# One decoder layer on one core: the first feed-forward bias added by four 32-row products, one per PSUM bank, in place of four whole ones

## The reference, cut to what matters

```
x = x + ffn(layernorm(x))
def bitlinear(x, w, b):
    xn = layer_norm(x)
    scale = 127 / clip(max|xn| over the row, 1e-5)
    xq = clip(round(xn * scale), -128, 127) / scale
    wq = clip(round(w / mean|w|), -1, 1) * mean|w|
    return xq @ wq.T + b
h = gelu(bitlinear(x, w1, b1))        # w1: 2048 x 512, b1: 2048
ffn = bitlinear(h, w2, b2)            # w2: 512 x 2048
```

## Time and profile before

| what | value |
|---|---|
| median of 3 runs | 994.33 us (993.60 to 994.83) |
| profiled execution, first to last instruction | 993.8 us |
| mean granted TensorE clock | 0.953 |
| TensorE busy | 907.3 us (91%) |
| VectorE busy | 788.4 us (79%) |
| ScalarE busy | 488.8 us (49%) |
| GpSimd busy | 148.4 us (15%) |

### The profile page before, as it was taken

How to read it: one execution, slowest core, us unless ns; L and a number is a source line. 1 busy time by engine, 2 the same in 40 slices (tenths; PEclk the granted TensorE clock), 3 DMA queues, 4 the chain that set the end, 5 groups by cost and what they waited for, 6 DMA issues and landing times.

```text
span 993.8 us, 18916 instructions
## 1 busy us (share of the span) xinstructions
PE 907.3 (91%) x7673; PEld 735.2 (74%) x7690; DVE 788.4 (79%) x1205; ACT 488.8 (49%) x687; POOL 148.4 (15%) x210
## 2 busy tenths in 40 slices
PE   3467999999989999999999989999999986989996
PEld 2357988988889888898989877788878854545552
DVE  4778978879788797888848666988889789889983
ACT  4445164361643615435152343545345346879994
POOL 3000111021110211101010200000000113324431
PEclk9589899999999999999997999999999988999999
DMA  9320102012020010200504033023320421322220
GB/s 247 105 72 32 44 12 95 13 33 65 12 92 16 33 65 11 66 21 33 172 12 159 1 128 107 23 108 127 127 93 34 160 76 34 106 85 96 96 75 32
DMA packets 36951, 72.47 MB, mean 73 GB/s; under 512 B 6466, under 2 KB 7234, under 8 KB 35850
## 3 DMA queue, kind: packets, MB, share of 16 engines
q1 hardware_dynamic: 35754, 68.29, 20.5%
q0 software_dynamic: 1120, 3.10, 1.2%
HBM read 57.76 MB, written 12.58 MB: 71 GB/s over the span
## 4 chain that ended last, share of the span: by engine, by line
PE 61%; issue 16%; DVE 15%; POOL 5%; ACT 2%; DMA 1%; SPq 0%; DVEq 0%; POOLq 0%; ACTq 0%
PE S L674 11%; PE P L62 7%; PE P L63 6%; PE P L64 6%; PE S L2153 4%; PE P L2143 4%; PE S L650 3%; POOL sm L370 3%; DVE E L1738 2%; DVE xf L919 2%; PE S L1599 2%; PE P L627 1%; PE P L751 1%; PE P L760 1%; PE S L1553 1%
## 5 line engine op out<-in xcount | busy, mean ns | idle before, releaser
L674 PE MATMUL S<-R,K 64*128 64x64 f32 x1792 | 117.7, 283 | 5.1 <-DVE K L965 2.8
L674 PEld LDWEIGHTS S<-R,K 64*128 64x128 f32 x1792 | 110.1, 196 | 16.2 <-issue 10.9
L370 POOL TENSOR_TENSOR sm<-sm,mhalf 128x16 f32<-128x16 f32 x8 | 30.6, 3827 | 280.4 <-DVE sm L1012 280.4
L2153 PE MATMUL S<-wq,hqT 128*128 128x512 bf16 x255 | 62.7, 392 | 5.0 <-ACT hqT L2086 5.0
L2143 PE MATMUL P<-wq,xqT 128*128 128x512 bf16 x240 | 64.6, 390 | 2.5 <-ACT xqT L2072 1.2
L919 DVE TENSOR_TENSOR xf<-P,xx 128x1024 f32<-128x1024 f32 x40 | 48.9, 1222 | 20.4 <-PE P L627 20.4
L1738 DVE TENSOR_SCALAR E<-S,upper 128x2048 f32<-128x2048 f32 x16 | 37.6, 2350 | 29.2 <-PE S L1586 29.0
L1744 DVE RECIPROCAL rec<-S 128x512 f32<-128x512 f32 x16 | 53.6, 3352 | 2.6 <-PE S L1601 2.5
L962 DVE TENSOR_TENSOR R<-R,D 128x256 f32<-128x256 f32 x96 | 41.1, 428 | 18.1 <-PE S L674 16.5
L1412 ACT ACTIVATE E<-E 128x2048 f32<-128x2048 f32 x16 | 30.6, 1914 | 43.8 <-DVE E L1738 43.8
L2153 PEld LDWEIGHTS S<-wq,hqT 128*128 128x128 bf16 x256 | 25.1, 101 | 34.0 <-ACT hqT L2086 5.1
(11 more groups left out here) (284 smaller groups left out, 2729.6 us busy)
## 6 DMA issues: line engine op xcount, KB each, us to landing
wch<-in_wff SPq DMA_DIRECT2D x32, 256.0 KB, 3.0
cwch<-in_wff SPq DMA_DIRECT2D x8, 1024.0 KB, 6.6
xt<-in_x SPq DMA_DIRECT2D x8, 512.0 KB, 4.5
y<-in_x SPq DMA_DIRECT2D x8, 512.0 KB, 3.9
out<-y SPq DMA_DIRECT2D x8, 512.0 KB, 3.3
cxt<-out SPq DMA_DIRECT2D x8, 512.0 KB, 4.1
ct<-in_ctx SPq DMA_DIRECT2D x8, 512.0 KB, 4.9
cxr<-out SPq DMA_DIRECT2D x8, 512.0 KB, 6.6
```

What stands on the lines that cost most here:

```text
L370: pool.tensor_tensor(sm[:, 2, :], sm[:, 1, :], mhalf[:, 0:2 * H], ALU.pow).then_inc(y_rstd, 1)
L674: mm = pe.matmul(ps[:, par, b, k, :], K[head_rows(par), r % 2, T * g:T * g + T], right_tokens(par, g, i), start=True, stop=True)
L2153: mm = pe.matmul(O[:, :], hqT[b % 2][:, k, :], w2q[:, k, :], start=k == 0, stop=k == NF - 1)
```

## The change

The bias rows are laid out four times. Row group n (partitions 32n to 32n+8) of `w1b` holds the pieces of b1 for the 512 columns of bank n, so `w1b` is 512 wide and not 2048; `pieces` has the nine pieces of the reciprocal scale at columns 32n to 32n+8 for each n. `product` first makes the 16 products with the ternary weights, and then four products of 32 rows, each for its own bank. The nine DMAs of `rows()` become 36, each with a quarter of the bytes.

```diff
-    w1b = sb("w1b", [P, FF], BF16)
+    w1b = sb("w1b", [P, C], BF16)
...
             for i in range(3):
                 for j in range(3):
-                    sp.dma_start(w1b[3 * i + j:3 * i + j + 1, :], b1p[j][:, :]).then_inc(rows_in, 16)
+                    for n in range(4):
+                        at = XD * n + 3 * i + j
+                        sp.dma_start(w1b[at:at + 1, :], b1p[j][XD * n:XD * n + XD, :]).then_inc(rows_in, 16)
...
-            pc, pr = pieces[f % 2], pres[f % 2]
+            pc, pr = pieces[f % 2][:, :], pres[f % 2]
...
-                pool.tensor_copy(pc[:, 3 * i:3 * i + 3], wide(pr[:, i:i + 1], [P, 3])).then_inc(s_piece, 1)
+                pool.tensor_copy(pc.rearrange("p (n c) -> p n c", n=4)[:, :, 3 * i:3 * i + 3], wide(pr[:, i:i + 1].unsqueeze(2), [P, 4, 3])).then_inc(s_piece, 1)
...
             if t == 0:
-                pe.wait_ge(rows_in, 9 * 16)
+                pe.wait_ge(rows_in, 36 * 16)
             pe.wait_ge(s_pT_ready, t + 1)
             for n in range(FF // C):
                 cols = slice(C * n, C * n + C)
                 for k in range(NC):
                     pe.matmul(Hp[:, cols], xqT[t % 2][:, k, :], w1q[:, k, cols], start=k == 0, stop=False)
-                mm = pe.matmul(Hp[:, cols], xqT[t % 2][:, NC, :], w1b[:, cols], start=False, stop=True)
+            for n in range(FF // C):
+                rows = slice(XD * n, XD * n + XD)
+                mm = pe.matmul(Hp[:, C * n:C * n + C], xqT[t % 2][rows, NC, :], w1b[rows, :], start=False, stop=True)
             mm.then_inc(s_h_done, 1)
```

## The result

| | before | after |
|---|---|---|
| median of 4 executions | 994.58 us (993.60 to 996.87) | 1019.62 us (1003.36 to 1500.87) |
| ratio | | 1.0122, 95% interval 1.0091 to 1.0153 |
| profiled execution, first to last instruction | 993.8 us | 1001.6 us |
| mean granted TensorE clock in it | 0.953 | 0.947 |

The account below looks back on a forecast made before the run. TensorE was taken to bound the chain around product(0) and, closely followed by another loop, the repeated steps. 993.8 span + 7.7 stall - 1.0 gain = 1000.5, with 0.5 to the median 1001.0 us; range 993.2 to 1002.5.

Parts of the forecast that it names:

- the sign: Whole kernel: slower, with a chance of 0.66.
- the stall's term: TensorE ahead of product(0): waits from 811.6 to 819.3 for the 36 DMAs, 7.7 us reaching the end in full.
- 7.7 - 1.0: Whole kernel: 7.7 us of stall less 1.0 us gained by TensorE's cheaper bias products.
- From the span to the time: Last step of the sum: the median lies 0.5 us above the profiled span, so 1000.5 becomes 1001.0.
- The issue's price: SyncE's queue: the 36 DMA issues start 0.64 us apart, as the nine did.
- the rivals with shorter issues: SyncE's queue: under 0.42 us apart, no stall, 993.3, chance 0.2; 0.42 to 0.58 apart, 993.3 to about 999, chance 0.17.
- 0.20 + 0.20 + 0.31: TensorE, each batch: two turns of 0.20 us and 0.31 for four 32-row products, against 0.86 removed.
- The rival that they are not side by side: TensorE's four 32-row products: 0.40 us more a batch, 1005.2 with the stall, chance 0.03.
- The steps: Repeated feed-forward steps: from 8.94 to about 8.90 us, limited by the ScalarE, VectorE and GpSimd loop; 0.3 us together.
- The rival "faster": Whole kernel: no stall and no turns worth the name, 992.9, or 992.2 if that loop gives way; deciding step 8.81, chance 0.05.
- The end of the program: Last feed-forward steps: they follow the ScalarE, VectorE and GpSimd loop already and give nothing.
- GpSimd and the queue behind the 36: GpSimd's zeroing and copies, and SyncE's later store and three loads, moved by 11 to 17 us: cost nothing.

Follow-up runs that it names:

- e1: The kernel after, unaltered, run once more (also written "again"): 1002.41 us, ratio 1.0057 to before.
- e3: The kernel before with its whole bias products, its nine DMAs cut into 36: 1006.53 us, ratio 1.0097 to before.
- e10: The kernel after with nine strided DMAs, the wait for the bias rows moved behind the 16 products: 992.91 us, ratio 0.9970 to before.
- e2: The kernel after with its 32-row products, but nine strided DMAs in place of 36: 992.88 us, ratio 0.9961 to before.
- e6: The kernel before, with ScalarE squaring only half of each centred row: 991.60 us, ratio 0.9960 to before.
- e7: e2 with ScalarE squaring only half of each centred row: 988.76 us, ratio 0.9936 to before.
- e9: The kernel after with 18 DMAs of two rows each in place of 36: 992.67 us, ratio 0.9975 to before.
- e5: The kernel after with its 36 DMAs, the wait for the bias rows moved behind the 16 products: 996.74 us, ratio 1.0026 to before.

## Why it came out as it did

The mechanism was the one predicted, and so was the sign. What failed is the size of the stall's term and what was added to it. The 36 DMAs were to cost 7.7 us, and they cost 9.2: 8.39 of stall and 0.84 behind it, which the prediction put at nothing. The span was to be 0.5 us from the time, and is 1.8. For the profiled execution this closes: 1001.0 + 1.3 from the span + 0.65 from the start of the stage + 1.4 up to `weigh` (8.78, where 7.7 - 0.35 = 7.35 was forecast) + 0.6 up to the third centring (0.29, where -0.35 was forecast) - 1.7 at the end of the program = 1003.3, and 1003.36 was measured, outside a range that ended at 1002.5. The median of the four, 1019.62, lies further out for the reason given with the result.

That e1 then stands 7.0 us above before (1002.41 - 995.45), where the prediction had 6.7 (7.7 - 1.0), is partly luck: terms that were too small by 1.4 us and a gain of 1.6 to 1.7 that was not foreseen stand against each other. Step by step:

- **From the span to the time.** "The median of the runs lies 0.5 above that span, so 1001.0." This step failed by itself. Every listed execution is 1.8 us longer than its span, so the profiled execution of before, with 993.8, took 995.6 and was a slowish one. Its 993.8 should have been carried to 995.6 + 6.7 = 1002.3 for such an execution. The later runs have before at 995.3 to 995.5, not 994.3.
- **The stall, 7.7 us.** It was 8.39 in again, 8.00 in e3. The 36 issues took 23.61 us, not 35 x 0.64 + 0.60 = 23.0: one of them in each run is long (1.42, and 1.11 in e3), the others start 0.63 apart as predicted. That one issue is the 0.6 by which the last starts later than forecast. The landing was 1.7 and not 2.0, but TensorE started only 0.25 behind it. What the sum left out altogether is the clock after it: `product(0)` starts at the lower level in e10 as in e1, but with the stall it stays there longer (in windows of 1 us, e1 is at 0.50 for the first 5 us and e10 for the first 3), and it takes 6.47 in place of 5.63 (whole products: 7.18 in place of 6.1). That term is 0.84 us; with it the 36 DMAs cost 8.39 + 0.84 = 9.2, and e1 against e2 measured 9.5.
- **The issue's price.** "I take 0.64 apart": right, and the rivals with shorter issues fell. A quarter of the bytes and of the source rows brought it from 0.60 to 0.59 and no further, so it doesn't go by the size here. The reason given, that it goes by the form (many partitions of SBUF into one), is weaker: into two or four rows it took 0.50 and 0.53.
- **The 32-row products.** "0.20 + 0.20 + 0.31" was 0.71 and measured 0.42, so TensorE gains 0.44 per batch and not 0.15 (20 x 0.216 = 4.32 to 3.88 us). Both terms were too large: the turn is 0.10 and not 0.20, and the four take one stream of 0.216 and not 0.31. The 0.20 was read from 64-row float32 products, and why a turn costs more there was not tried. But two rows of the prediction had 0.10 already: `weigh` begins 0.31 after a product with a stream of 0.216, and the 32-row products 0.21 after one of 256 columns, whose stream is about half as long, 0.108. The rival that they are not side by side fell.
- **The steps.** 8.94 to 8.91, as predicted, and for the reason given: e6 and e7 show TensorE able to do 8.67 when the other loop is shorter. The waits went to `gm` as predicted and to `fxm` as well. The rival "faster", which needed 8.81, fell.
- **The end of the program.** "The last steps follow that loop already and give nothing." This was wrong by 1.69 us in after. The final 16 products stood at the lower clock in before and in e3 and at full clock in after, in e1, in e9 and in e10. But the 16 of the batch before them turn the other way. TensorE's timeline in before, and the chain of e10:

```profile
977.35 3.40 PE L2153 MATMUL S<-wq,hqT 128*128 128x512 bf16 x15 [3.02 <-ACT hqT L2086]
982.14 1.07 PE L2130 MATMUL S<-identb,gm 128*128 128x128 bf16 x16 [1.39 <-DVE gm L2240]
```

```profile
977.55 6.44 PE S L2156 x16
983.99 0.91 PE S L2131 x16
...
986.85 3.64 PE S L2156 x16
```

In before they are done 1.4 us ahead of `gm`, and nothing waits for them; in e10 they take 6.44 and lie on the chain. So of the 1.69 only 0.44 is left in e10, and 0.46 in e9 (17.23 - 16.77). What the narrow products bring in e10, the start of the stage set aside, is 0.49 - 0.04 + 0.18 - 0.14 + 0.44 = 0.9 us, the 1.0 of the forecast. The 2.4 to 2.6 by which the medians of e9 and e10 lie below before aren't explained by that: the profiled execution of e10 is the slowest of its eight (995.58), and that of e9 the fastest of its nine (990.89), with 2.66 of its gain between the first and the third centring, where `product(2)` runs at full clock (3.62 us for its 16 whole products, 5.30 in e10). That the narrow products cause the change of level is not shown; e6_half_before, with whole products and an earlier end, has its final 16 at full clock as well.
- **GpSimd and the queue behind the 36.** Nothing, as predicted: the store left at 819.30, three loads followed, and no reader waited for them (`fxr` was read at 837.89).

Open is this: the kernels with narrow products scatter more (e10's executions lie from 990.37 to 995.58, those of before beside it from 993.98 to 996.67), and what decides in which of them `product(2)` is at full clock (26.44 us to the third centring in e9, 28.92 in e10) was not tried.

## What to carry to other kernels

Before an edit multiplies DMAs on a queue, count issue times from the moment at which their data are ready to the moment at which the first reader comes: 18 issues fitted into those 17 us and were free, 36 did not and cost 9. The remedy is fewer issues (one strided DMA for rows of the same source) or a wait placed behind the work that doesn't need the data. "DMA: Bandwidth & Descriptors" of the Trainium skill, Rules for kernel authors, says the first too: many small transfers are to be made into one. The runs agree, with 9.5 us between 36 and nine. Small-row products are worth grouping by their shape, since each change of shape costs 0.10 us, and a gain on one engine should be held against the loop next to it before it is multiplied by the number of steps.

## What the runs showed of the hardware that was not expected

- One DMA from 128 partitions of SBUF into four rows is issued in 0.53 us, from 64 into two rows in 0.504, but from 32 into one row in 0.59, and from 128 into one row in 0.60: more rows to write did not cost more.
- One of the 36 issues took 1.42, 1.42, 1.11 and 1.58 us in the four traces that have them (after, e1, e3, e5), the median 0.59.
- Four 32-row products of 512 columns side by side, with a turn on each side, cost 0.42 us, and so did a single one.
- 16 products of 512 columns took 3.63 us at a granted clock of 1.00, 5.31 at 0.69 and 6.44 at 0.54: which level a short burst meets moved the end of after by 1.7 us, more than the 1.0 us that the edit was to save, and the level of the burst before it gave most of that back in e9 and e10.
